# Giving the first layer's softmax exponentials a per-partition bias column in a two-layer transformer kernel

## What is computed

```
xn = layernorm(x)
q, k, v = xn @ Wq + bq, xn @ Wk + bk, xn @ Wv + bv    # 32 query heads, 8 key heads, 8 channels each
q, k = rope(q), rope(k)
scores = q @ k.T / sqrt(8)                            # a key after its query: -inf
attn = softmax(scores, axis=-1)
x = x + (attn @ v) @ Wo + bo + ffn0(xn)
x = x + attention1(layernorm(x)) + ffn1(layernorm(x)) # second layer: 16 heads x 16 heads within a token
```

## Time and profile before

| what | us |
|---|---|
| median of 3 runs (626.23 to 629.3) | 626.25 |
| the profiled execution's own time | 626.23 |
| its span in the profile | 624.5 |
| PE busy | 570.9 (91%) |
| ACT busy | 488.0 (78%) |
| DVE busy | 441.5 (71%) |
| POOL busy | 268.6 (43%) |

### The profile page before, as it was taken

One profiled execution on the slowest core, in us unless ns is written; L12 is line 12 of the kernel. 1 busy time (PEld: TensorE's weight loads), 2 busy tenths in 40 slices (PEclk: granted clock), 3 DMA queues, 4 the chain that ended last, 5 costly groups with the idle time before them and its releaser, 6 DMA issues. The chain is left out here.

```text
span 624.5 us, 13580 instructions
## 1 busy us (share of the span) xinstructions
PE 570.9 (91%) x5085; PEld 291.6 (47%) x5085; DVE 441.5 (71%) x903; ACT 488.0 (78%) x925; POOL 268.6 (43%) x380
## 2 busy tenths in 40 slices
PE   3697899989999999999999999999999999998882
PEld 1333434425455545555453445555444452555661
DVE  6899789878597667867887676665565553577563
ACT  2488899978988998999987897979998988844330
POOL 4776566364334228613985563253152410613000
PEclk9799899989999999999999999999999999999997
DMA  8801101030404030221301004440504004044540
GB/s 285 296 2 35 31 5 34 2 51 2 69 17 62 27 52 1 41 39 18 52 1 36 1 1 68 60 65 6 86 2 69 8 2 68 27 78 85 85 53 30
DMA packets 150920, 30.45 MB, mean 49 GB/s; under 512 B 133952, under 2 KB 149568, under 8 KB 150848
## 3 DMA queue, kind: packets, MB, share of 16 engines
q1 hardware_dynamic: 150272, 29.19, 23.5%
q10 hardware_dynamic: 576, 0.33, 0.2%
HBM read 19.02 MB, written 10.49 MB: 47 GB/s over the span
## 5 line engine op out<-in xcount | busy, mean ns | idle before, releaser
L904 ACT ACTIVATE Pt<-psS 128x512 f32<-128x512 f32 x576 | 299.0, 622 | 33.2 <-PE psS L655 28.1
L669 PE MATMUL psV<-Pt,vaug 128*32 128x512 f32 x1152 | 150.1, 608 | 3.2 <-POOL Pt L1539 2.9
L1539 POOL TENSOR_SCALAR_AFFINE_SELECT Pt<-Pt 128x512 f32<-128x512 f32 x128 | 90.9, 746 | 62.0 <-ACT Pt L904 61.9
L655 PE MATMUL psS<-qTf,kTf 32*128 32x512 f16 x576 | 73.6, 387 | 5.2 <-DVE kTf L1158 1.9
L655 PEld LDWEIGHTS psS<-qTf,kTf 32*128 32x128 f16 x576 | 20.0, 91 | 83.2 <-ACT Pt L904 46.9
L1594 POOL TENSOR_TENSOR ss<-ss,mhalf 128x1 f32<-128x1 f32 x16 | 9.0, 565 | 93.7 <-DVE ss L1383 93.7
L669 PEld LDWEIGHTS psV<-Pt,vaug 128*32 128x32 f32 x1152 | 25.4, 108 | 46.8 <-issue 30.4
L954 ACT ACTIVATE stage<-psS 128x512 f32<-128x512 f32 x64 | 33.1, 606 | 10.6 <-PE psS L772 10.5
L1585 POOL TENSOR_TENSOR r<-qk,cos 128x256 f32<-128x256 f32 x16 | 14.5, 904 | 50.6 <-ACT qk L938 49.2
L1389 DVE SCALAR_TENSOR_TENSOR qtmp<-qtmp,ss 128x1024 f16<-128x1024 f32 x16 | 22.1, 1378 | 13.3 <-ACT qtmp L974 13.2
L1520 POOL TENSOR_TENSOR rt<-qkv,cs 128x320 f32<-128x320 f32 x16 | 16.6, 1035 | 33.8 <-DVE qkv L1119 26.1
(11 more groups left out here) (351 smaller groups left out, 1262.9 us busy)
## 6 DMA issues: line engine op xcount, KB each, us to landing
qkvscr<-rqkv SPq DMA_DIRECT2D x16, 384.0 KB, 2.7
G<-qkvscr SPq DMA_DIRECT2D x48, 128.0 KB, 3.7
stage<-in_wg SPq DMA_DIRECT2D x4, 512.0 KB, 7.2
oscr<-o SPq DMA_DIRECT2D x16, 128.0 KB, 3.0
at<-oscr SPq DMA_DIRECT2D x16, 128.0 KB, 2.1
out<-yout SPq DMA_DIRECT2D x16, 128.0 KB, 3.0
x<-in_x SPq DMA_DIRECT2D x1, 1536.0 KB, 12.0
r<-in_wgu SPq DMA_DIRECT2D x2, 512.0 KB, 7.3
```

Source lines behind the costliest of these rows:

```text
L655: e.matmul(psS[j][:], kd[32 * j:32 * j + k, h, 128 * at:128 * at + 128], qd[32 * j:32 * j + k, 4 * h:4 * h + 4, :].rearrange("p s n -> p ( ...
L669: ins = e.matmul(psV[32 * j:32 * j + 32, :], vaug[:, at, j, 32 * h:32 * h + 32], Pt[(4 * Q + j) % NP][:], start=(kb == 0 and h == 0), stop ...
L904: e.activation(Pt[u % NP][:], psS[j][:], ACT.Exp, scale=SC0 / UP / UP).then_inc(S["exp"], 1)
L1539: e.affine_select(out=p, in_=p, pattern=[[0, 4], [1, 128]], compare_op=ALU.is_ge, fill=0.0, base=0, channel_multiplier=-1).then_inc(S["mas ...
```

## The change

Each first-layer exponential of the first pass gets `bias=low[:]`, a column of 128 x 1 in SBUF, where it had no bias argument and so a constant 0.0 inside the instruction. The column holds `SC0 * SHIFT`, which is -45.25 / sqrt(8) = -16.0, so each exponential and each sum is smaller by a factor of e^16. POOL's stage `zero` fills the column with one more memset, the third of now six instructions, so the counts of later waits on it go up by one; ACT waits for it once, ahead of the first exponential. `LOW` goes from 1e-36 to 1e-32. The second pass's own exponentials are as they were. The new tile takes 32 bytes per partition between `QXf` and `widest`, so `widest`, `Pt` and all tiles that are laid out after them start 32 bytes higher.

```
-LOW, HIGH, LARGE = 1e-36, 1e30, 3e38
+LOW, HIGH, LARGE = 1e-32, 1e30, 3e38
+SHIFT = -45.25
...
         QX = [flat(QXf[:]).bitcast(F16)[:, 1280 * i:1280 * i + 1280].rearrange("p (h c) -> p h c", c=32) for i in range(2)]
+        low = sb("low", [128, 1])
         widest = sb("widest", [128, NT])
...
             def ts(m):
                 j, h = divmod(m, 2)
-                w.wait_ge("zero", 5)
+                w.wait_ge("zero", 6)
...
             def exp(Q):
                 n = QUADS[Q][0]
+                w.wait_ge("zero", 3)
                 for j in range(4):
                     u = 4 * Q + j
                     w.wait_ge("qk", u + 1)
                     w.wait_ge("pv", (u - NP) // 4 + 1)
                     if n < NT:
-                        e.activation(Pt[u % NP][:], psS[j][:], ACT.Exp, scale=SC0 / UP / UP).then_inc(S["exp"], 1)
+                        e.activation(Pt[u % NP][:], psS[j][:], ACT.Exp, bias=low[:], scale=SC0 / UP / UP).then_inc(S["exp"], 1)
...
                 e.memset(hpi[:], float(np.pi / 2)).then_inc(S["zero"], 1)
+                e.memset(low[:], SC0 * SHIFT).then_inc(S["zero"], 1)
                 e.memset(blockb[:], 0.0).then_inc(S["zero"], 1)
-                w.wait_ge("zero", 3)
+                w.wait_ge("zero", 4)
                 for p in range(2):
                     e.memset(blockb[64 * p:64 * p + 64, 64 * p:64 * p + 64], 1.0).then_inc(S["zero"], 1)
-                    w.wait_ge("zero", 4 + p)
+                    w.wait_ge("zero", 5 + p)
```

## The result

| kernel | median us | range, runs | span of the profiled execution |
|---|---|---|---|
| before | 626.24 | 625.12 to 629.3, 4 | 624.5 |
| with the change | 651.39 | 650.25 to 651.46, 4 | 649.2 |

The ratio is 1.039, with a 95% interval of 1.0351 to 1.0428: 25.2 us slower. 654 had been forecast, between 636 and 674. Of the 53 executions of the kernel before that stand beside the experiments, one took 1351.52 us, about twice the others, is in none of the ratios and left no profile, so whether it went through the second pass is open.

What follows compares the result with a forecast made beforehand. PE was taken as the bound from 80 to 520 us (98% busy), ACT next at 88%. Span 624.5 plus 28 for the column, other parts nothing, plus 1.7 around the span gave 654 us, range 636 to 674.

Steps and rivals of the forecast that it cites:

- 90 ns an exponential: Column's price on ACT, from start-to-start distances of 128x1024 ACTIVATEs with and without a scale column; 51.8 us over 576 exponentials.
- The 75 ns of sine and cosine: Lower price for the column, from durations of a sine without (257 ns) and a cosine with one (332 ns).
- working (a): ACT from 25 to 545 us, cut into 5 us stretches: added work overflowing each stretch's room sums to about 22 us.
- (b): PE's 90 weight-load waits ended by an exponential, each 0.36 us later: 32 us on the path.
- PE's share: PE's busy share from 80 to 520 us, forecast to fall from 98% to about 93 or 94%.
- The memset and the wait: POOL's extra memset, covered by over 10 us, and ACT's wait before the first exponential, long met: nothing added.
- The 32 bytes: Moved start of Pt and later tiles; sizes, strides and instruction count stay: nothing taken, 1 us kept to either side.
- 1: Rival at the exponentials: column costs nothing on the path, distance stays 0.48 us, time 626; chance 0.07.
- 2: Rival at ACT: price paid but idle time takes most of it, 3 to 12 us added, 629 to 638; chance 0.12.
- 3: Rival at ACT: whole 51.8 us on the path or more, 678; chance 0.14 together with the PE clock rival, 4.
- 4: Rival at PE: short stalls make its clock fall, ten dips adding 15 us, 669; chance 0.14 together with 3.
- 5: Rival: the flag sends the kernel through the second pass over 16 tiles, above 1200 us; chance 0.01.

Runs made afterwards that it cites:

- e4_two_columns: The changed kernel with the bias column as SBUF's last tile, and the exponentials' scale given as a second column: 688.02 us, ratio 1.1001.
- e8_change_again: The changed kernel measured once more, unaltered, on the same chip as three other follow-up runs: 650.83 us, ratio 1.0414 to the kernel before.
- e1_low_last: The changed kernel with the bias column laid out as SBUF's last tile, so no other tile moves: 650.59 us, ratio 1.0396 to the kernel before.
- e12_work_between: As e7_work_elsewhere, but ACT's copy stands ahead of each quad's fourth exponential instead of behind the quad: 648.18 us, ratio 1.0386.
- e11_last_column: The changed kernel with the bias column only on each quad's fourth exponential, the others taking the constant, column as last tile: 628.11 us, ratio 1.0068.
- e7_work_elsewhere: As e3_immediate, plus an ACT copy of 128x330 numbers to an unread tile behind each quad's four exponentials: 638.88 us, ratio 1.0221.
- e3_immediate: The kernel before with the shift as a constant inside the exponential and LOW at 1e-32, no column, no memset: 624.82 us, ratio 1.000.
- e2_pad32: The kernel before with an unused 32-byte tile ahead of widest, moving the tiles as in the change, no column: 626.62 us, ratio 1.0031.
- e5_g3_moved: The kernel before with an unused 32-byte tile on each side of G3, so G3 starts at an odd multiple of 32 bytes: 626.48 us, ratio 1.0024.
- e9_pad64: The kernel before with an unused tile of 64 bytes per partition ahead of widest, G3 still at a multiple of 64: 624.73 us, ratio 0.9998.

## Why the prediction was right, point by point

**The price.** 90 ns an exponential, from the distance behind a 128x1024 with a scale column. The exponentials' distance grew by 92 ns, although their data comes from PSUM and they have half the length: the price is by instruction. That the two came so near is partly luck, since the two rows differ in more than the column: one writes f16 and has an exponential behind it, the other writes bf16 and has an accumulator read. ACT's busy time was forecast near 539 us and is 535.1. The 75 ns of sine and cosine was the worse row: it compares single durations, the sine's own right behind a load of tables. The Trainium skill (page "ScalarE: Activation LUTs", section "What ACT_TABLE_LOAD costs") says about 93 ns for each pointer operand; the two columns of e4_two_columns, at 94 and 97 ns in duration, agree.

**The share.** 28 us forecast, 25 measured, between working (a) with 22 and (b) with 32. The total is better than its parts: all 28 us were to come ahead of the last exponential, at 572 us, where 21.5 came (21.7 in e8_change_again, 23.9 in e1_low_last), and 3.2 came behind it, where nothing was forecast. So the step that led from 22 up to 28 ("two engines that are then both some 93% busy" lose room that (a) counts as usable) was too high, and the 3.2 us, 2.1 of which come with PE's clock as shown below, made up for half of it. (a) was nearer, and its one free choice, the length of the stretch, was a little too long; the 22 also depends on where the first stretch starts, which moves it from 17 to 22 (at the starts that the prediction names it comes to 21). At one quad, 3.6 us, the same working gives 24.9 and follows the measured curve of 3.8, 9.3, 25.3 and 62.7 us for 13, 26, 53 and 106 us of added work. (b) was too high, as it had said itself, since it prices every wait at the full 0.36 us. But its picture, that PE is late because the fourth bank is late, is the one that e12_work_between and e11_last_column bear out, and (a) alone is blind to it: it would give e7_work_elsewhere 25 us as well, where 13.9 were measured. That (a) is right for the column is then partly luck: in these runs it fits where all of the added work lies ahead of the release.

**PE's share.** I forecast 93 or 94% in the dense stretch; the profile shows 96%, and e1_low_last, whose trace has all matmuls, 97% (425.1 of 440 us). That sign failed although the time is longer, and the page of the profile of e1_low_last shows why, beside the earlier trace rows:

```profile
PE 589.2 (91%) x5085; PEld 296.5 (46%) x5085; DVE 439.3 (68%) x903; ACT 535.1 (82%) x925; POOL 263.9 (41%) x381
```

The same 5085 matmuls are busy for 589.2 us where they were for 570.9, 18.3 us of the 25. The clock accounts for less than 4 of them: its mean was 0.975 over 649.8 us, against 0.980 over 624.5. So most of the delay is inside what counts as busy, and a falling busy share is a poor sign of a matmul engine that is held up.

**What was costed at nothing.** The memset and the wait: no run has them without a column, but nothing of them shows. The first exponential starts at 26.9 us in the change and at 27.1 in e3_immediate, which has neither. The 32 bytes: I had kept 1 us to either side, and here the step from "sizes, strides and the count of instructions stay" to "take nothing" was too light. The move slows the 48 loads of G by some 1.5 us each in the median. Most are issued early enough; the last ones lie on the chain that ends last, and alone the move costs 1.3 to 1.5 us. My own sign for it had been that nothing outside the dense stretch moves by more than 1 us, and the end moved by 3.2 us in the profiled execution of the change (1.1 in e8_change_again). The two traces of this one kernel show what the larger figure holds beside the loads. Here is each from its last exponential to its end, the change first (us; busy PE, PEld, DVE, ACT, POOL; granted clock; DMA share):

```profile
566.10:649.20 83.10, 62.33 (x649) 43.41 (x652) 50.01 (x108) 26.79 (x46) 9.83 (x17) 0.91 0.53 62
```
```profile
566.30:647.30 81.00, 59.20 (x648) 41.60 (x652) 49.96 (x108) 26.77 (x46) 9.81 (x17) 0.95 0.54 64
```

The loads are as slow in both (5.3 us), and the other 2.1 us come with the clock: in the first it was at 1.2 GHz from 613.9 to 617.3 us and from 624.2 to 627.6, in the second it stayed at 2.4 GHz up to 639.4. PE had stood idle for 1.06 us shortly before the first fall (up to 613.45 us), but in the second trace as well (up to 613.79 us), so what brought the clock down in the one and not in the other is open. e1_low_last, with `G3` in its old place, has one such stretch behind its last exponential, a clock of 0.93 there and an end of 81.3 us.

**The rivals.** 1 fell with the distance of 0.57 us. 2 and 3 fell with 25 us; e4_two_columns shows what 3 would have needed, twice the price. 4: the clock was 1.00 from 80 to 520 us, though 99 of the 132 waits of weight loads for an exponential lie there, so the Trainium skill's rule on short idle times, which the prediction sets beside this rival, did not show in that stretch. 5: no second pass ran in the change, as the time alone tells.

## What to carry to other kernels

A constant that is the same for all partitions belongs inside the ACT instruction, not in a column in SBUF: here the column cost 92 ns on each of 576 instructions and 25 us in all, the immediate nothing. What added work on an engine that is 88% busy costs could be read off the trace of before in this kernel, once its idle time was counted over stretches as long as the buffers reach (here one quad), not over the whole; and work behind the last release of the shared banks cost 13.9 us where the same work ahead of it cost 23.8. When a small tile is added in the middle of a layout, look at the start of every tile that a DMA fills in short pieces.

## What the runs showed of the hardware that I had not expected

A load of 128 KB in pieces of 64 bytes took 3.7 us with the tile at a multiple of 64 bytes (two starts) and 5.2 us with it at an odd multiple of 32 (one start) (e2_pad32, e5_g3_moved against e9_pad64); writing out from tiles moved in the same way changed little (2.7 to 2.8 us for the 384 KB ones in the change). And an ACTIVATE pays for each column on its own: 0.48, 0.57 and 0.66 us from start to start for none, one and two. And PE's busy time grew by 18 us for the same matmuls when it was held up by another engine (e1_low_last), so it is no measure of PE's work.
